# Attention slots of a fused adaLN block: score tiles in two groups, softmax reciprocals spread through DRAM

## What is computed

```python
q = rotary_embedding(q, seq_len, HEAD_DIM)
k = rotary_embedding(k, seq_len, HEAD_DIM)
scale = 1.0 / jnp.sqrt(jnp.asarray(HEAD_DIM, dtype=x.dtype))
scores = jnp.einsum('bqhd,bkhd->bhqk', q, k) * scale
mask = jnp.tril(jnp.ones((seq_len, seq_len), dtype=bool))[None, None, :, :]
scores = jnp.where(mask, scores, NEG_INF)
weights = jax.nn.softmax(scores, axis=-1)
out = jnp.einsum('bhqk,bkhd->bqhd', weights, v)
out = out.reshape(batch, seq_len, NUM_HEADS * HEAD_DIM)
return jnp.einsum('bsf,fe->bse', out, W_out)
```

## Time and profile before

| | us |
|---|---|
| three runs, median (lowest to highest) | 996.21 (993.32 to 998.24) |
| the profiled execution, its time | 990.0 |
| its span, first to last instruction | 988.2 |
| PE busy | 903.2 (91%) |
| DVE, ACT, POOL busy | 770.1, 743.5, 570.8 |
| mean granted clock of PE | 0.978 of 2.4 GHz |

### The profile page before, as it was taken

How to read it: one execution, slowest core, us unless ns; L and a number is a source line. 1 busy time by engine, 2 the same in 40 slices (tenths; PEclk the granted TensorE clock), 3 DMA queues, 4 the chain that set the end, 5 groups by cost and what they waited for, 6 DMA issues and landing times. The chain is left out here.

```text
span 988.2 us, 21752 instructions
## 1 busy us (share of the span) xinstructions
PE 903.2 (91%) x6278; PEld 657.7 (67%) x6278; DVE 770.1 (78%) x2328; ACT 743.5 (75%) x2070; POOL 570.8 (58%) x687
## 2 busy tenths in 40 slices
PE   4699999999999999999999999999999878999920
PEld 3467667676776677777767677677676556888820
DVE  7577777777877787877778778777887679899847
ACT  4488878878787887788778878787878755777725
POOL 1445456645666467657765764657566356765532
PEclk9999999999999999999999999999999989999975
DMA  8234443334344434433343344343333357999844
GB/s 258 84 94 105 111 110 98 95 94 105 95 111 117 116 97 119 118 97 95 109 114 96 102 122 119 101 114 112 106 94 96 98 199 269 311 317 331 296 143 128
DMA packets 124580, 135.78 MB, mean 137 GB/s; under 512 B 13837, under 2 KB 108443, under 8 KB 120496
## 3 DMA queue, kind: packets, MB, share of 16 engines
q1 hardware_dynamic: 118768, 122.61, 42.8%
q0 software_dynamic: 4544, 8.93, 2.7%
q10 hardware_dynamic: 1152, 2.85, 0.8%
HBM read 51.72 MB, written 39.49 MB: 92 GB/s over the span
## 5 line engine op out<-in xcount | busy, mean ns | idle before, releaser
L1357 POOL TENSOR_TENSOR four<-four 128x512 f32<-128x512 f32 x128 | 161.2, 1280 | 276.1 <-DMA four<-four 138.8
L1276 DVE CUSTOM_DVE_ANT_0 ps<-ps,tri 128x512 f32<-128x512 f32 (+3 forms) x512 | 239.0, 520 | 73.2 <-PE ps L1070 73.1
L1172 ACT ACTIVATE prob<-ps,nmax 128x512 f32<-128x512 f32 (+3 forms) x512 | 264.7, 534 | 4.1 <-DVE nmax L1276 3.3
L1091 PE MATMUL ps<-ident,prob 128*128 128x128 f32 x1280 | 191.1, 279 | 6.5 <-ACT prob L1172 2.4
L1091 PEld LDWEIGHTS ps<-ident,prob 128*128 128x128 f32 x1280 | 142.8, 141 | 55.5 <-ACT prob L1172 26.4
L1361 POOL TENSOR_TENSOR qk_lo<-four,qk_hi 128x512 fp32r<-128x512 f32 x128 | 163.1, 1296 | 0.1
L1193 ACT COPY probt<-ps 128x512 f32<-128x512 f32 (+2 forms) x256 | 125.2, 522 | 41.1 <-PE ps L1091 41.1
L1113 PE MATMUL ps<-probt,val 128*64 128x512 f32 (+3 forms) x1024 | 152.0, 439 | 0.2 <-ACT probt L1193 0.2
L1200 ACT CAST qk_hi<-four 128x512 fp32r<-128x512 f32 x128 | 79.4, 620 | 94.3 <-POOL four L1357 92.8
L1263 DVE TENSOR_TENSOR four<-ps,turn_s 128x1024 f32<-128x1024 f32 x64 | 78.4, 1225 | 54.8 <-PE ps L1035 50.3
L1113 PEld LDWEIGHTS ps<-probt,val 128*64 128x64 f32 x1024 | 67.8, 136 | 73.7 <-issue 59.5
(11 more groups left out here) (276 smaller groups left out, 2234.9 us busy)
## 6 DMA issues: line engine op xcount, KB each, us to landing
four<-four SPq DMA_DIRECT2D x252, 128.0 KB
wt<-parts SPq DMA_DIRECT2D x24, 1024.0 KB, 6.7
slots<-fill SPq DMA_DIRECT2D x64, 288.0 KB, 2.8
parts<-split SPq DMA_DIRECT2D x64, 128.0 KB, 2.3
wq_lo<-parts SPq DMA_DIRECT2D x6, 1024.0 KB, 6.3
hb<-h_hi SPq DMA_DIRECT2D x64, 64.0 KB, 2.3
hb<-h_lo SPq DMA_DIRECT2D x64, 64.0 KB, 2.0
plain<-results SPq DMA_DIRECT2D x8, 512.0 KB, 7.5
```

The source lines that it names most:

```text
L1091: mm = e.transpose(ps[:, PT + at % 2, at_block * P:(at_block + 1) * P], prob[:, unit, kk * P:(kk + 1) * P], ident[:])
L1172: e.activation(prob[:, unit, 0:w], ps[:, bank_s(idx) + j, 0:w], ACT.Exp, bias=nmax[:, q.par, idx, j:j + 1], scale=-1.0, accum_out=den[:, q ...
L1276: e.tensor_tensor_reduce(block_, block_, tri[:, S - w:S], -1.0, HIGHEST, ALU.add, ALU.min, nmax[:, q.par, idx, j:j + 1]).then_inc(v_max, 1)
L1357: e.tensor_tensor(qk[:, cols], tt[:, cols], ur[:, cols], op=ALU.add).then_inc(g_qk, 1)
```

## The change

pe_qk is cut into pe_k and pe_q. PE's slot goes k, turns 0 and 2a, the turn of the reciprocals, q, turns 2b and 1, scores 0 and 1, values, scores 2 and 3, turns 3a and 3b, out, v, routing. All eight exponentials of a pair are now taken in one slot. DVE stores 3a and 3b, ACT the other four; DVE's reciprocals move to the end of the slot in which the pair is q1. The eight columns of reciprocals lie in a 128 x 128 tile of ones, which one transpose turns into a free quarter of bank 7; ACT copies 8 partitions of it; SP writes them to DRAM (sp_sums) and reads them back with each row spread over 64 partitions, one DMA per head (sp_spread). The order of den's columns changes with it.

```diff
             def pe_turn_sum(e, q):
-                e.wait_ge(a_rep, q.n + 1)
-                e.wait_ge(v_tk, min(q.n + 3, STEPS))
-                for i in range(TB):
-                    mm = e.transpose(ps[:, W1, i * P:(i + 1) * P],
-                                     rrep[:, i, :, :].rearrange("p j f -> p (j f)"), ident[:])
-                mm.then_inc(p_r, 1)
+
+                e.wait_ge(v_rden, q.n + 1)
+                if q.n == 0:
+                    e.wait_ge(s_rden, 1)
+                e.transpose(ps[:, PT + 1, 3 * P:4 * P], rden[:], ident[:]).then_inc(p_r, 1)
...
                 if q0.live:
-                    pe_qk(e, q0)
+                    pe_k(e, q0)
                 if q2.live:
                     spare_read(e, i, c - 1)
                     pe_turn_prob(e, q2, "0")
                     pe_turn_prob(e, q2, "2a")
-                if q1.live:
-                    pe_scores(e, q1, 0)
+                    pe_turn_sum(e, q2)
+                if q0.live:
+                    pe_q(e, q0)
                 if q2.live:
                     pe_turn_prob(e, q2, "2b")
                     pe_turn_prob(e, q2, "1")
-                    pe_turn_sum(e, q2)
                 if q1.live:
+                    pe_scores(e, q1, 0)
                     pe_scores(e, q1, 1)
                 if q2.live:
                     pe_values(e, q2)
                 if q1.live:
+                    pe_scores(e, q1, 2)
+                    pe_scores(e, q1, 3)
                     pe_turn_prob(e, q1, "3a")
-                    pe_scores(e, q1, 2)
+                    pe_turn_prob(e, q1, "3b")
                 if q2.live:
                     pe_out(e, q2)
-                if q1.live:
-                    pe_turn_prob(e, q1, "3b")
                 if v.live:
                     pe_v(e, v)
                 if c in SPARE:
                     if q1.live:
-                        e.wait_ge(a_ev, 4 * q1.n + 1)
+                        e.wait_ge(v_ev, 2 * q1.n + 1)
                     elif q2.live:
-                        e.wait_ge(v_ev, 2 * q2.n + 2)
+                        e.wait_ge(a_ev, 4 * q2.n + 3)
                     route_pe(e, i, c)
-                if q1.live:
-                    pe_scores(e, q1, 3)
...
             def act_r(e, q):
                 e.wait_ge(p_r, q.n + 1)
                 if due(q.n):
-                    e.wait_ge(v_ot, q.n)
-                e.copy(rs[:], ps[:, W1, :]).then_inc(a_r, 1)
...
+                    e.wait_ge(d_rt, 16 * q.n)
+                e.copy(rt8[:], ps[0:NU, PT + 1, 3 * P:4 * P]).then_inc(a_r, 1)
...
                 if q2.live:
-                    act_exp(e, q2, 5)
-                    act_exp(e, q2, 6)
-                    act_exp(e, q2, 7)
                     act_store(e, q2, "0")
+                    act_r(e, q2)
                     act_store(e, q2, "2a")
-                    act_rep(e, q2)
+                    act_store(e, q2, "2b")
                     act_store(e, q2, "1")
-                    act_r(e, q2)
...
                     act_exp(e, q1, 3)
-                    act_store(e, q1, "3a")
                 route_act_part(e, i, c, 1)
...
+                if q1.live:
+                    for unit in range(4, NU):
+                        act_exp(e, q1, unit)
                 if q0.live:
                     act_hi(e, q0, 1)
-                    act_hi(e, q0, 0)
                 if v.live and (i, c) != (0, 2):
                     act_v(e, v)
+                if q0.live:
+                    act_hi(e, q0, 0)
...
             def dve_ot(e, q):
                 n = q.n
                 e.wait_ge(p_vp, n + 1)
-                e.wait_ge(a_r, n + 1)
+                e.wait_ge(d_rs, 32 * (n + 1))
...
                 if q2.live:
                     dve_ot(e, q2)
                 if q1.live:
-                    dve_peak(e, q1, 4)
-                    dve_peak(e, q1, 5)
+                    for unit in range(4, NU):
+                        dve_peak(e, q1, unit)
                 if q2.live:
                     dve_acc(e, q2)
                 if q1.live:
+                    dve_store(e, q1, "3a")
                     dve_store(e, q1, "3b")
+                    dve_rden(e, q1)
                 route_dve_last(e, i, c)
...
+            def sp_sums(e, q):
+
+                e.wait_ge(a_r, q.n + 1)
+                if due(q.n):
+                    e.wait_ge(d_rs, 32 * q.n)
+                e.dma_start(recips, rt8[:]).then_inc(d_rt, 16)
+
+            def sp_spread(e, q):
+                e.wait_ge(d_rt, 16 * (q.n + 1))
+                if due(q.n):
+                    e.wait_ge(v_ot, q.n)
+                for j in range(2):
+                    e.dma_start(rs[j * HD:(j + 1) * HD, :], recips[j * TB:(j + 1) * TB, :].rearrange("i q -> (i q)")
+                                .partition_broadcast(HD)).then_inc(d_rs, 16)
...
                 if v.live:
                     sp_h(e, v)
+                if q2.live:
+                    sp_sums(e, q2)
                 if q0.live:
 
                     load_turn(e, q0, MOVES[:2] if q0.n < 2 else MOVES)
+                if q2.live:
+                    sp_spread(e, q2)
                 route_sp(e, i, c)
```

More of the change, by code:

```diff
@@ L89, in adaln_kernel @@
 def adaln_kernel(nc, x_in, w_qkv, w_out, gate_w, expert_bias, w_up, w_down, c_t, w_mod,
-                 cos_in, sin_in, ident_in, tri_in, rank_in, const_in, out, xs, ys, parts, gates):
+                 cos_in, sin_in, ident_in, tri_in, rank_in, const_in, out, xs, ys, parts, gates, recips):
     ctx = ExitStack()
@@ L978, in adaln_kernel @@
             den = sb(ph, "den", [P, 2, NU])
-            rden = sb(ph, "rden", [P, NU])
-            rrep = sb(ph, "rrep", [P, TB, 2, HD])
+            rden = sb(ph, "rden", [P, P])
+            rt8 = sb(ph, "rt8", [NU, P])
             wog = sb(ph, "wog", [P, E])
@@ L1016, in cols_of, with pe_k @@
                 return slice(b * S, (b + 1) * S)
-            def pe_qk(e, q):
+            def pe_k(e, q):
                 n = q.n
@@ L1030, in pe_qk, with pe_q @@
                 e.matmul(ps[:, W1, :], wq_hi[:, k_cols], h_lo[:, cols_of(q.b)], start=False, stop=True)
+            def pe_q(e, q):
+                n = q.n
                 e.wait_ge(a_v, min(n + 2, NV))
@@ L1078, in pe_turn_prob @@
                 if u == "3a":
-                    if due(2 * n):
-                        e.wait_ge(v_ev, 2 * n)
+                    if due(4 * n - 1):
+                        e.wait_ge(a_ev, 4 * n - 1)
                 elif u == "3b":
@@ L1083, in pe_turn_prob @@
                         e.wait_ge(a_ev, 4 * n)
-                elif u == "2a":
-                    e.wait_ge(v_ev, 2 * n + 1)
+                elif u in ("0", "2a"):
+                    e.wait_ge(v_ev, 2 * n + {"0": 1, "2a": 2}[u])
                 else:
-                    e.wait_ge(a_ev, 4 * n + {"0": 1, "2b": 2, "1": 3}[u])
+                    e.wait_ge(a_ev, 4 * n + {"2b": 1, "1": 2}[u])
                 at_block = 0
@@ L1109, in pe_values @@
                 e.wait_ge(v_t, min(n + 3, STEPS))
+                e.wait_ge(v_tk, min(n + 3, STEPS))
                 v, first = val[q.group], (q.hp % GP) * P
@@ L1189, in act_store @@
                 e.wait_ge(p_t, 6 * n + TURNS.index(u) + 1)
-                if u == "3a" and due(n - 1):
-                    e.wait_ge(p_vp, n - 1)
                 dst, src = turned(q, u)
@@ L1281, in dve_rden @@
                 if due(q.n):
-                    e.wait_ge(a_rep, q.n)
-                e.reciprocal(rden[:], den[:, q.par, :]).then_inc(v_rden, 1)
+                    e.wait_ge(p_r, q.n)
+                else:
+                    e.wait_ge(s_rden, 1)
+                e.reciprocal(rden[:, 0:NU], den[:, q.par, :]).then_inc(v_rden, 1)
             def dve_store(e, q, u):
@@ L1287, in dve_store @@
                 e.wait_ge(p_t, 6 * n + TURNS.index(u) + 1)
-                if u == "3b" and due(n - 1):
+                if u == "3a" and due(n - 1):
                     e.wait_ge(p_vp, n - 1)
@@ L1323, in dve_slot @@
                     n_factors(e)
-                if q2.live:
-                    dve_store(e, q2, "2b")
                 if q1.live:
-                    dve_peak(e, q1, 0)
-                    dve_peak(e, q1, 1)
-                    dve_peak(e, q1, 2)
-                    dve_peak(e, q1, 3)
+                    for unit in range(4):
+                        dve_peak(e, q1, unit)
                 route_dve(e, i, c)
@@ L1442, in _ @@
                 def _(e):
+                    e.memset(rden[:], 1.0).then_inc(s_rden, 1)
                     e.wait_ge(d_late, 64)
@@ L2035 @@
     args += [nc.dram_tensor("slots", (SLOTS, ROW), F32).ap(), nc.dram_tensor("results", (2 * B * S, E), F32).ap(),
-             nc.dram_tensor("parts", (P, NX * 4 * I), F32).ap(), nc.dram_tensor("gates", (B, E), F32).ap()]
+             nc.dram_tensor("parts", (P, NX * 4 * I), F32).ap(), nc.dram_tensor("gates", (B, E), F32).ap(),
+             nc.dram_tensor("recips", (NU, P), F32).ap()]
```

22 lines of the change are left out of this document (4 added, 18 removed).

## The result

The changed kernel takes **1169.5 us** (median of four runs, 1166.1 to 1173.6), the kernel before 995.9; the ratio is 1.175 (95% interval 1.170 to 1.179). It is slower, as forecast, but by 174 us and not by 116: outside the range of 1056 to 1155. The profiled execution took 1169.16 us with a span of 1167.3.

A forecast was written before the change was run, and what follows sets the result against it. PE set the pace before; the change was to close a ring over the spread: 12.78 us per slot against 11.71, +66 us, plus 50 for routing, on 990.0, with the median 6 above: 1112 us, range 1056 to 1155.

The forecast's parts named there:

- the ring: Attention slot: ot, DVE's stores and reciprocals, transpose, q, turn, rotation and next spread wait in a closed loop, 12.78 us.
- turn to ot: Slot's leg from the turn's start to ot's start: turn 1.23, spread's landing 5.8, hand-over to DVE 0.05 us.
- ot to the turn: Slot's leg from ot's start: DVE's work to the reciprocals' end 4.6 us, then transpose and q to the turn's start 1.1.
- routing: Slots with routing work: PE waits for DVE's store 3a or ACT's last routing operation, so q starts later; 50 us in all.
- the landing of the spread: Load queue: second spread, issued behind four rotation transfers, lands 5.8 us after the turn's end; bounds 5.3 and 7.6.
- rival D: PE in the attention: granted clock falls to its 1.2 GHz level, PE's 9 us per slot double, over 1300 us; 3%.
- Rival C: Spread's read or the queue takes 1 us more through DRAM and contention: 13.8 us per slot, 1174 us; 10%.
- Rival A: Spread lands under the value product, ot waits for nothing new, PE gives its 1.0 us per slot: 928 us, median 934; 5%.

The follow-up runs named there:

- e1: Changed kernel with the load queue issuing the two spreads ahead of the rotation's four transfers; 1059 us, 1.030 of the kernel before.
- e2: Changed kernel with ot multiplied by a constant tile, so nothing on DVE waits for the spread; 1052 us (kernel before on that chip: 1027).
- e3: Changed kernel with q's matmuls directly behind k's, ahead of the turns; 1157 us (kernel before on that chip: 1027).
- e4: Changed kernel with one more 128 KB spread, never read, between the rotation and the two spreads; 1260 us (kernel before on that chip: 1027).
- e5: Changed kernel with each spread writing 32 partitions instead of 64, 64 KB instead of 128; 1108 us (kernel before on that chip: 994).
- e6: Changed kernel with 16 more transposes on PE ahead of out, their result overwritten; 1161 us (kernel before on that chip: 994).
- e9: Changed kernel with ot multiplied by a constant, q's cosine product ahead of k's and 3a's store ahead of the residual; 1012 us (kernel before: 1028).
- e7: e1 with DVE's cosine product of q ahead of k's and the store of 3a ahead of the residual; 1010 us, 1.013 of the kernel before.

## Why the prediction was right and where it was wrong

**The mechanism was right.** ot waits for the spread, the spread for the rotation's issues, the rotation for the turn, the turn for q, q for the reciprocals' transpose, that for DVE's last operation of the slot before. e1 opens the ring by one exchange, e2 by taking the wait away, e3 opens it at another place in part, e4 stretches it. DVE idles 2.4 us before ot, ended by rs<-recips, as the text said one would see.

**The sum, term by term.** Forecast 13.59 per slot (12.78 and 0.81 of routing, 50 us over 62 slots), measured 14.49:

| term | forecast | measured |
|---|---|---|
| turn to ot (turn 1.23, landing 5.8, hand-over) | 7.08 | 7.81 |
| ot to the turn, slots without routing or its wait | 5.70 | 5.75 |
| routing, mean over all slots at the full clock | 0.81 | 0.70 |
| low clock, mean over all slots | 0 | 0.23 |

**The step that failed is the landing of the spread, "I take 5.8, near the clean end, since most slots of before show no late rotation".** It was wrong twice. "A load of 64 KB from DRAM lands 2.2 after its issue starts" gave the lower end for a read of 128 KB, which takes 2.9 (3.1 in the mean); e5 with 64 KB measures 2.1 and brings the leg to 6.96. And late slots are not rare: in the changed kernel the two spread issues take their usual 1.2 us in 43 of 61 slots, where the second lands 6.2 us after the turn's end, and longer in 18, where it lands 7.1 after it. Even the undisturbed slots are above 5.8. In the kernel before, the last rotation transfer already landed more than 5 us after the turn's end in 24 of 61 slots. The page of before had a row of the spread's size, a write to DRAM:

```profile
parts<-split SPq DMA_DIRECT2D x64, 128.0 KB, 2.3
```

So a row of the same size would not have given 2.9 either; what is shown is the price of this read, and that half of it costs 0.8 less. The bounds 5.3 and 7.6 held the mean, 7.81 - 1.28 = 6.5, but the value was taken near the wrong end. 0.73 x 61 = 45 us, most of the 57 by which the time was missed.

**The second step is rival D, which I gave 3%.** "Gaps stay under 2 us" was no reason, and not so: PE waits up to 2.7 us at 'out', and the clock fell 14 times in the attention. It did not double PE's 9 us everywhere but cost 0.23 x 61 = 14 us. It was no rival of the forecast but a part of it: by e6 the waits that the forecast itself foresaw brought most of it about.

**Routing** came out at 0.70 for 0.81. The turn of 0 did wait for ACT's copy in slots with c = 0, 3 and 5: ot to the turn is 7.25, 7.05 and 7.25 there (medians) against 5.75, so 1.5, 1.3 and 1.5 where 1.6 was forecast.

**Rival C** gave 1174 and came nearest by its number. Its condition, a read of one line by 64 partitions that takes 1 us more than the earlier trace rows, was met in kind: 2.9 us in the median and 3.1 in the mean instead of 2.2. But its mechanism alone does not give the time: the landing was 0.7 and not 1.0 over my value, and the clock made up part of the rest. The rule cited of the Trainium skill ("DMA: Bandwidth & Descriptors", Latency and other measured facts), 0.2 us for an access on average and 2 at high load, decides nothing here: the write of the reciprocals lands 0.9 after its issue ends, and no run shows a DRAM access that is slow by itself. What made a spread late was the read itself, as e5 prices it, and the issues ahead of it, as e1 and e4 price them.

**Rival A** (928) priced what PE would give. It is wrong as a price: e2 and e9 show 12.09 and 11.50 with the spread out of the way, not 10.7. That PE's own sum fits inside the ring was true; that the time would fall to it otherwise was not. The new order puts q, the cosine product and the value product so close behind each other that the last waits for their bank, and ot to the turn is 1.0 longer than before even in e2.

## What to carry to other kernels

A transfer on an in-order queue waits for all that the queue issues before it. If it serves an older stage than its neighbours, put it ahead of them, and follow the dependences once round the slot: work that is off the path in time can still close a ring by its place in three queues. Price a transfer by a row of its own size, direction and pattern, or call its price open, and take the mean of the landings, not a clean slot; and when a forecast has PE waiting once per slot, ask what the granted clock does.

## What the runs showed of the hardware

**The time at the low clock grows with PE's waiting, roughly.** With PE's order as in the changed kernel, the time at the 1.2 GHz level in the attention goes up with the period: 0 at 12.1 (e2), 3 at 12.3, 20 at 13.6, 61 at 14.5, 140 us at 15.5 per slot, where PE is busy for 89, 88, 82, 79 and 76% of the attention. The kernel before has 99% and none, and e3 fits with 32 us at 13.9 and 82%. It is no strict rule: e7 has 10 us in three falls at 12.0 per slot and 92%, and e2 none. In a stretch at the low clock a 512-wide matmul follows the last after 0.42 us instead of 0.23:

```profile
205.92 0.63 PE L1037 MATMUL ps<-h_hi,wq_lo 128*128 128x512 f32 x1
...
206.34 0.63 PE L1038 MATMUL ps<-h_lo,wq_hi 128*128 128x512 f32 x1
```

**Late rotations go with the fetching of instructions.** The page lists two instruction queues (q8 and q14, packets of 8 and 16 KB), counted on the same 16 DMA engines. In the changed kernel 33 of 61 rotations have such a packet starting between 0.2 us before the turn's end and 4.4 after it; their last transfer lands 5.17 after the turn's end in the mean. The 28 others land after 4.29, most of them between 4.20 and 4.30. In the kernel before it is 5.19 (35 slots) against 4.44 (26). The load queue's own issue of the spreads can be late as well; the slot at 556.61 against the one shown above:

```profile
556.61 1.22 DVE L1254 TENSOR_TENSOR four<-ps,turn_s 128x1024 f32<-128x1024 f32 x1 [1.73 <-PE ps L1038]
...
557.86 2.48 SPq L1370 DMA_DIRECT2D four<-four  x4
...
560.43 2.50 SPq L1384 DMA_DIRECT2D rs<-recips  x2
...
565.34 0.69 DVE L1292 TENSOR_TENSOR ot<-ps,rs 128x512 f32<-128x512 f32 x1 [3.97 <-DMA rs<-recips]
```

Two issues take 2.50 us instead of 1.18, and ot starts 8.73 after the turn instead of 7.32. That the fetch is the cause was not tried by a run of its own; it is a coincidence of times.

**The rest of the kernel differs by chip.** From the last turn to the end the traced kernels take 225 to 233 us on two chips and 259 to 266 on two others; each kernel was traced on one kind of chip only. That the chip is behind it, and not the edits, rests on the kernel before, which takes 994 to 996 us on the first kind and 1027 to 1028 on the second.
